# Layer 1 of a two-layer graph network: four additions of a turn made together on VectorE, and a one-hot tile written by ScalarE two groups ahead

## The reference

```python
h = jnp.maximum(_layernorm(x), 0.0)
x_u = data @ var_u;  x_v = data @ -var_u
logits = x_u[edge_src] + x_v[edge_dst] + var_c
q = jax.nn.softmax(logits, axis=-1)                  # over the 8 heads
x_sep = data[edge_dst] * edge_vals[:, None]
for m in range(8):
    agg = jax.ops.segment_sum(q[:, m:m + 1] * x_sep, edge_src, num_segments=3125)
    y = y + agg @ var_w[m]
return y + var_b
```

## Time and profile before

| | before |
|---|---|
| median of 3 runs | 2374.38 us (2373.89 to 2381.76) |
| profiled execution, its own time | 2375.3 us |
| its span in the profile | 2373.6 us |
| layer 0's loop, about | 60 to 1060 us |
| layer 1's loop, about | 1200 to 2350 us |

### The profile page before, as it was taken

The page is one execution under the profiler, slowest core; times in us unless marked ns, Lnnn a source line. Parts: engine busy times, 40 slices in busy tenths (PEclk is TensorE's granted clock), DMA queues, the critical chain, the costliest instruction groups (busy, mean ns, idle before and its releaser), DMA issues.

```text
span 2373.6 us, 53585 instructions
## 1 busy us (share of the span) xinstructions
PE 1700.9 (72%) x10041; PEld 1192.6 (50%) x10041; DVE 1422.4 (60%) x6161; ACT 555.3 (23%) x1979; POOL 1625.3 (68%) x1700
## 2 busy tenths in 40 slices
PE   5698888899899989989845555555655555565554
PEld 5455555555555555556434444444444444444444
DVE  5334434444434444343358888788888888888885
ACT  2233333333333333332111111111111111111110
POOL 2777777777777777774456766667676766767673
PEclk7799999988989898898555555555555555555555
DMA  2544444444444444442133333333333333333332
GB/s 68 120 99 100 96 97 99 98 94 96 100 93 102 98 98 95 96 103 52 38 109 90 94 90 93 89 91 93 91 92 92 92 90 90 94 90 92 92 91 57
DMA packets 353203, 216.99 MB, mean 91 GB/s; under 512 B 284700, under 2 KB 325751, under 8 KB 352926
## 3 DMA queue, kind: packets, MB, share of 16 engines
q0 software_dynamic: 66800, 113.26, 21.0%
q1 hardware_dynamic: 284692, 102.18, 17.9%
q10 hardware_dynamic: 1684, 1.24, 0.2%
HBM read 209.80 MB, written 6.69 MB: 91 GB/s over the span
## 4 chain that ended last, share of the span: by engine, by line
DVE 28%; issue 25%; POOL 17%; PE 16%; DVEq 7%; DMA 6%; ACT 1%; POOLq 0%; SPq 0%; ACTq 0%
POOL X L581 16%; DMA X<-table_src,slot_s 4%; DVE EQW L1134 4%; DVE EQW L1140 3%; DVEq L1199 3%; PE bank L1363 3%; PE bank L1346 2%; DVE EX L1180 2%; DVE OT L976 2%; DVE r L1172 2%; DVE r L1176 2%; PE bank L1372 2%; DVE r L1167 2%; PE bank L1354 2%; DVE OE L1185 2%
## 5 line engine op out<-in xcount | busy, mean ns | idle before, releaser
L589 POOL DMA_INDIRECT G<-table_node_and_list,slot_s x825 | 796.1, 965 | 378.5 <-issue 210.6
L581 POOL DMA_INDIRECT X<-table_src,slot_s x825 | 789.6, 957 | 295.3 <-issue 234.4
L1482 PE MATMUL bank<-Q,G 125*64 125x128 f32 x1650 | 414.9, 424 | 183.6 <-DVE Q L1193 183.6
L1482 PEld LDWEIGHTS bank<-Q,G 125*64 125x64 f32 x1650 | 313.7, 221 | 196.4 <-issue 125.9
L1346 PE MATMUL bank<-filler 128*128 128x384 bf16 x1100 | 377.1, 343 | 1.6 <-issue 1.6
L990 DVE TENSOR_TENSOR sT<-sT,bank 65x16 f32 x275 | 46.2, 168 | 551.7 <-PE bank L1382 513.6
L1493 PE MATMUL bank<-R,w_z 65*64 65x64 f32 x1104 | 133.9, 316 | 278.2 <-DVE sT L1201 278.2
L976 DVE TENSOR_SCALAR OT<-KBT,base_p 48x375 bf16<-48x375 int32 x550 | 231.7, 422 | 65.6 <-issue 35.2
L1493 PEld LDWEIGHTS bank<-R,w_z 65*64 65x64 f32 x1104 | 122.9, 224 | 282.5 <-issue 281.2
L1363 PE MATMUL bank<-XT,w_ex 128*64 128x375 f32 x550 | 254.3, 547 | 7.5 <-issue 7.5
L1372 PEld LDWEIGHTS bank<-w,H 65*125 65x125 f32 x1650 | 232.3, 200 | 0.0
(11 more groups left out here) (168 smaller groups left out, 2072.5 us busy)
## 6 DMA issues: line engine op xcount, KB each, us to landing
KBT<-in_dst SPq DMA_DIRECT2D x550, 70.3 KB, 2.1
X<-in_edge_attr SPq DMA_DIRECT2D x275, 93.8 KB
HK<-keys SPq DMA_DIRECT2D x275, 93.8 KB
X<-table_src,slot_s POOLq DMA_INDIRECT x825
G<-table_node_and_list,slot_s POOLq DMA_INDIRECT x825
BW<-table_dst_parts SPq DMA_DIRECT2D x275, 6.0 KB
UW<-table_logit_src_parts SPq DMA_DIRECT2D x275, 0.8 KB, 1.7
table_node_and_list<-sm SPq DMA_DIRECT2D x1, 1562.5 KB
```

The lines of the kernel that those rows point to most:

```text
L581: pool.indirect_dma_start(X[:, j, q, D:2 * D], None, tA, bass.IndirectOffsetOnAxis(ap=slot_s[:, j, q:q + 1], axis=0)).then_inc(gat_a[0][j] ...
L589: pool.indirect_dma_start(G[:, j, q, :], None, tH, bass.IndirectOffsetOnAxis(ap=slot_s[:, j, q:q + 1], axis=0)).then_inc(g_gather[j], 16)
L1482: last = pe.matmul(bank[2 + j % 2][0:D, 0:WM], G[0:P, j, q, 0:D], Q[:, j % 2, q].rearrange("p m n -> p (m n)"), start=(q == 0), stop=(q == ...
```

## The change

1. `add_outputs` is called once in a turn, at j = 0, as the last step of the slot. It first makes the value loads of all four groups of the turn (t - 2) and then their four additions; each addition still waits for the one before.
2. The comparison of `window_t` in layer 1 moves from DVE to ACT. ACT writes `OD = |node - KBT|` (48 x 375, float, one buffer) and then `OT = relu(1 - OD)`, which is 1 where both agree and 0 elsewhere. Both come last in ACT's slot and are for group g + 2. The steps for groups 0 and 1 stand ahead of the loop.
3. SP's load of `KBT` waits for the first of the two (`u_D`) in place of `u_OT`. Layer 0 keeps its window on DVE.

```diff
             def rows1w(t, j):
                 g = RB * t + j
-                done(sp, u_OT, t, j, RB)
+                done(sp, u_D, t, j, RB)
...
+            def window1_t(t, j):
+                act.wait_ge(kbt_load[1][j], (t + 1) * 16)
+                done(act, u_OT, t, j, 1)
+                act.activation(OD[:], KBT[:, j, :], ACT.Abs, bias=base_p[:, bass.ds(RB * t + j, 1)], scale=-1.0
+                               ).then_inc(u_D, 1)
+
+            def window1_one(t, j):
+                done(act, u_D, t, j)
+                done(act, u_U, t, j, RB)
+                act.activation(OT[:, j, :], OD[:], ACT.Relu, bias=one_col[:, 0:1], scale=-1.0).then_inc(u_OT, 1)
...
             def body1w(t, j):
                 back(exps_w, t, j, 1)
                 back(neighbours_w, t, j, 2)
+                back(window1_t, t, j, -2)
+                back(window1_one, t, j, -2)
...
+            for j in range(2):
+                window1_t(0, j)
+                window1_one(0, j)
...
             def add_outputs(t, j):
+                own = [j for j in range(RB) if not isinstance(t, int) or RB * t + j < NG]
                 dve.wait_ge(u_y, t + 1)
-                done(dve, u_acc, t, j, 1)
-                first = dve.value_load(first_of[0:1, bass.ds(RB * t + j, 1)], min_val=0, max_val=N - WG)
-                to = yT[:, bass.ds(first, WG)]
-                dve.tensor_tensor(to, to, bank[6][0:D, j * WG:(j + 1) * WG], ALU.add).then_inc(u_acc, 1)
+                firsts = [dve.value_load(first_of[0:1, bass.ds(RB * t + j, 1)], min_val=0, max_val=N - WG) for j in own]
+                for j, first in zip(own, firsts):
+                    done(dve, u_acc, t, j, 1)
+                    to = yT[:, bass.ds(first, WG)]
+                    dve.tensor_tensor(to, to, bank[6][0:D, j * WG:(j + 1) * WG], ALU.add).then_inc(u_acc, 1)
...
             def body1w(t, j):
 
-                back(lambda t, j: window_t(1, t, j), t, j, 0)
                 back(window_places, t, j, 2)
-                back(add_outputs, t, j, 2 * RB)
                 back(exp_sums, t, j, 2)
...
                 back(logits_less_max, t, j, 1)
+                if j == 0:
+                    back(add_outputs, t, j, 2 * RB)
```

More of the change, by code:

```diff
@@ L169, in build_gnn @@
         KBT = sb("KBT", [WP, RB, GE], I32)
+        OD = sb("OD", [WP, GE])
+        one_col = sb("one_col", [WP, 1])
         OT = sb("OT", [WP, RB, GE], BF16)
@@ L266, in build_gnn @@
                                     "scale", "head", "OH"))
+        u_D = sem("u_D")
         u_Q, u_agg, u_R, u_y, u_acc = (sem(f"u_{n}") for n in ("Q", "agg", "R", "y", "acc"))
@@ L872, in _ @@
             dve.memset(eps_col[:], EPS)
+            dve.memset(one_col[:], 1.0)
             dve.memset(no_key[:], -1.0)
@@ L971, in group0, with window_t @@
                                 ).then_inc(dve_g[0], 1)
-            def window_t(l, t, j):
-                dve.wait_ge(kbt_load[l][j], (t + 1) * 16)
-                done(dve, (f_h1, u_U)[l], t, j, RB)
+            def window_t(t, j):
+                dve.wait_ge(kbt_load[0][j], (t + 1) * 16)
+                done(dve, f_h1, t, j, RB)
                 dve.tensor_scalar(OT[:, j, :], KBT[:, j, :], base_p[:, bass.ds(RB * t + j, 1)], None,
-                                  ALU.is_equal).then_inc((f_OT, u_OT)[l], 1)
+                                  ALU.is_equal).then_inc(f_OT, 1)
             def window_e(t, j):
@@ L1004, in body0w @@
             def body0w(t, j):
-                back(lambda t, j: window_t(0, t, j), t, j, 0)
+                back(window_t, t, j, 0)
                 back(same_next, t, j, 2)
```

## The result

The changed kernel takes 2417.70 us (median of 4, 2414.68 to 2419.34) against 2374.14 us (median of 4, with the runs of before that were made beside it). The ratio is 1.018, 95% interval 1.0157 to 1.0204: slower by 43.6 us, well outside the 0.5% that can't be told from nothing. The span of the profiled execution is 2417.6 us.

What follows compares the result with a forecast made beforehand. DVE with its sequencer was taken as the bound. A turn of 12.18 + 1.41 + 3.85 = 17.44 us against 16.59, 67 times +0.85, adds 57 us to 2374.4: 2431 us, range 2390 to 2475.

Steps and rivals of the forecast that it cites:

- What bounds the kernel: Layer 1's loop: DVE's datapath and sequencer set the 16.59 us turn; PE's 4.1 us wait for additions bounds nothing.
- The window leaves DVE: DVE's three gaps without additions, L1158 to L1163, become 0.47 us each, ended by the exponential; upper bound 0.60.
- signs of being wrong: New profile: loads closer than 0.5 us, DVE waiting over 0.1 us a slot for gathers or exponential, branch period below 16.
- The window comes to ACT: ACT's queue: two more instructions, 0.22 to 0.477 us each, ACT working 1.1 to 1.65 us a slot, at no price.
- The cover of 2 us: ACT's idle time before the next exponential: about 3 us left, one taken by the window instructions, so 2 us spare.
- ACT comes late: Rival: window instructions delay ACT's exponential, each short gap growing up to 1.0 us, up to 2630 us; chance 0.06.
- The additions go together: DVE's long gap: loads 0.71 us each, 0.72 to the first addition, additions 0.30 apart; 3.85 us in all.
- Sum: Whole turn of layer 1's loop: 17.44 us in place of 16.59, +0.85, 67 times, +57 us.
- the list of signs: New profile if right: branch every 17.4 us, loads 0.7 us, additions 0.30 apart, gaps 0.47, POOL waiting 2 us a turn.
- Overlapping loads: Rival: four loads cost DVE's sequencer little more than one, long gap 2.0 us, turn 15.6, 2307 us; chance 0.11.
- That gain and loss cancel: Rival: the window's saving on DVE offsets the grouped loads, long gap 3.0 to 3.15 us, 2363 to 2386 us; chance 0.06.

Runs made afterwards that it cites:

- e2: Kernel before with the four additions together at the end of slot 0, window still on DVE; 2465.8 us, 1.0378 of the kernel before.
- e1: Changed kernel with additions back to one a slot in their old place, window on ACT; 2375.0 us, 1.0001 of the kernel before.
- e3: Changed kernel with all four value loads made twice, the second set used; 2590.2 us, 1.090 of the kernel before.
- e6: Changed kernel with additions spread one, one and two over slots 3, 0 and 1; 2338.0 us, 0.9842 of the kernel before.
- e10: Changed kernel with four spread load-addition pairs: behind Q and at slot end, in slots 3, 0 and 1; 2311.6 us, 0.9745 of the kernel before.
- e7: e1 with ACT's two window instructions moved ahead of the row numbers and the copy to R; 2333.1 us, 0.9821 of the kernel before.
- e8: e7 with the addition of slot 0 moved behind the weights Q; 2341.2 us, 0.9869 of the kernel before.
- e5: Changed kernel without value loads and additions in layer 1, so its results are left out; 2270.4 us, 0.9565 of the kernel before.
- e4: Changed kernel with value loads given no bounds, which moved the comparisons to the additions' addresses; 2435.6 us, 1.025 of the kernel before.

## Why the prediction was right

The forecast was 2431 us within 2390 to 2475, slower; measured were 2417.7 us. By its steps:

- **What bounds the kernel.** That DVE with its sequencer is the bound and PE's 4.1 us wait bounds nothing was right for the kernel before: the changed kernel has no such wait and is slower, and e2 has DVE's window and no such wait either and takes 18.01 us a turn. The margin was 0.42 us in one slot of the turn, which the prediction did not look at.
- **The window leaves DVE.** The three short gaps were to be 0.47 and are 0.46, 0.47 and 0.46 us, ended by the exponential. One of the signs of being wrong was a wait for it of more than 0.1 us a slot: it is 0.17 us in 128 slots, in half of them, and 0.08 on average. That sign was set too tight, since this wait is the gap that was forecast.
- **The window comes to ACT.** The two instructions take 0.61 us each, above the 0.48 of the nearest row that was the upper end. With them ACT works 1.9 us in a slot, where 1.65 was the upper end. ACT still had room: in the turn shown it stands idle for at least 1.25 us before each exponential. The cover of 2 us had been read from a slot in which ACT was not held; in the slot of PE's wait the kernel before had none. It was real only together with the grouping: e1 has the same ACT work without it and loses 1.03 us a turn. The rival "ACT comes late" described a real mechanism. It did not come true in the changed kernel because the grouped additions free PE.
- **The additions go together.** 0.71 us a load, 0.72 to the first addition, 0.30 between additions: measured 0.71 to 0.72, 0.73 and 0.30. The first load starts 0.29 us before L1178 (1704.60 against 1704.89), not 0.1. That is the largest miss among the terms, at its bound; 0.24 and not 0.2 from the last addition to the sum goes the other way. So the long gap is 3.71 in place of 3.85 us.
- **Sum.** 17.44 us a turn forecast, 17.28 measured; +57 us forecast, +43.6 measured. The stretches that the change leaves alone are the same to 0.01. The sum also said that POOL's wait for row numbers goes away, while the list of signs had 2 us a turn; the signs were right, with 1.94. As POOL is not the bound here, this changes nothing in the time.
- **The rivals.** Overlapping loads are ruled out by the chain of waits and by e3. That gain and loss cancel is wrong here by 44 us. ACT did not come late in the changed kernel, but did in e1.

What the prediction did not see is what e1 showed: the two halves of the change are not independent. Alone, the window's move is worth nothing (2375.0), the grouping costs 1.39 us a turn (e2), and together they cost 0.66, less than the sum of both. All kernels here that are faster and compute everything have the window on ACT and no four loads in a row, and either additions that do not make PE wait for long (e6, e10) or a window that stands ahead of that wait in ACT's queue (e7, e8). No run has the additions placed as in e6 or e10 and the window on DVE, so what the spacing is worth by itself is not shown.

Open is how far e10 can go: 0.57 us a turn lie between it and e5, whose turn has no additions at all. In e10 POOL has no gap of more than 0.3 us between gathers either, since its gathers take 1.00 us on average (0.95 in e5, both from 1300 to 2200 us); why they are longer there is open, and so is whether a faster DVE would still gain anything.

## What to carry to other kernels

Scalar loads into an engine's registers are serial work of its sequencer, and cost what no datapath work covers: count them before collecting them in one place. Spread, each did best in front of a wait that was there anyway (0.22 to 0.24 us with its addition), and cost more behind a long instruction in a stretch without a wait (0.54 to 0.64). A long wait on an engine off the critical path need not be a gain to be had, but it is no free room either: before work is moved into a queue behind it, look at what that queue does while it waits. And when a change has two halves, run each alone, since here one half was worth nothing without part of the other.

## What the runs showed of the hardware

- One bounded value load in DVE's sequencer takes 0.71 us in the loop (load 0.30, bounds 0.19, assert 0.02, address 0.06, steps of 0.03 to 0.04 between them), and the bounds' part is as long when it comes 2 us after the load (e4).
- Leaving out the bounds of a value load moved the comparisons to its use and added a second assert; for four additions in a row this cost 0.23 us a turn (e4).
- Four loads of addresses that were already formed cost 0.62 us each (e3).
- ACT's Abs and Relu over 48 x 375 elements, with a scale and a bias from a tile, took 0.61 us each, the Relu from PSUM over 64 x 375 with neither 0.48 us.
- POOL's gather instruction took 0.94 us at the least and up to 1.32 us in e10; the mean from 1300 to 2200 us was 0.95 us in e5 and 1.00 us in e10, with 0.30 us between two of them. What makes some longer is open.
